# Two transformer layers on one core: the routing of the second mixture of experts moved into the second attention's loop

## Time and profile before

| what | value |
|---|---|
| median of 3 runs | 2520.67 us (2514.0 to 2524.66) |
| the profiled execution | 2512.72 us, its span 2511.0 us |
| layer0 | 0 to about 599 us |
| attention1 | about 600 to 1863 us, first scores at 619 us |
| route1 | about 1863 to 2126 us |
| experts1, combine1 | about 2127 to 2431 us, then to 2511 us |
| PE clock granted, mean | 0.92 of 2.4 GHz |

### The profile page before, as it was taken

How to read it: one execution, slowest core, us unless ns; L and a number is a source line. 1 busy time by engine, 2 the same in 40 slices (tenths; PEclk the granted TensorE clock), 3 DMA queues, 4 the chain that set the end, 5 groups by cost and what they waited for, 6 DMA issues and landing times. The chain is left out here.

```text
span 2511.0 us, 67688 instructions
## 1 busy us (share of the span) xinstructions
PE 2272.6 (91%) x16828; PEld 1709.2 (68%) x16829; DVE 1888.3 (75%) x6162; ACT 1605.6 (64%) x4162; POOL 1015.9 (40%) x1979
## 2 busy tenths in 40 slices
PE   5999999997999999999999999999989991999960
PEld 3777777774666666666666666666657771999960
DVE  6888888871888888888888888888864552666658
ACT  2555555553777777777777777777753331667664
POOL 5676676671222222222222222222213666555542
PEclk9999999997999999999999999999985555999985
DMA  1011001001000000000000000000021111222225
GB/s 33 28 31 33 30 29 33 27 26 47 1 0 0 0 0 0 0 0 0 0 0 0 0 0 0 0 0 0 0 70 61 58 62 52 57 60 60 61 69 168
DMA packets 77583, 68.83 MB, mean 27 GB/s; under 512 B 10573, under 2 KB 70490, under 8 KB 77036
## 3 DMA queue, kind: packets, MB, share of 16 engines
q1 hardware_dynamic: 68830, 50.88, 6.9%
q0 software_dynamic: 8704, 17.39, 2.1%
HBM read 33.55 MB, written 22.62 MB: 22 GB/s over the span
## 5 line engine op out<-in xcount | busy, mean ns | idle before, releaser
L1017 DVE SCALAR_TENSOR_TENSOR restT<-ps_t,leadT 128x512 f16<-128x512 f32 (+1 forms) x768 | 462.8, 603 | 147.3 <-ACT leadT L978 95.3
L892 PE MATMUL ps_s<-xT_all,qm 128*128 (+1 forms) x1024 | 492.8, 563 | 11.8 <-issue 10.9
L978 ACT ACTIVATE leadT<-ps_t 128x512 f16<-128x512 f32 (+1 forms) x768 | 400.4, 522 | 151.0 <-PE ps_t L908 151.0
L908 PEld LDWEIGHTS ps_t<-ident,p 128*128 128x128 f32 x2560 | 320.8, 141 | 216.4 <-issue 180.9
L908 PE MATMUL ps_t<-ident,p 128*128 128x128 f32 x2560 | 405.4, 273 | 1.2 <-DVE restT L1017 0.5
L846 POOL CAST v_parts<-v_all 128x36 bf16 (+1 forms) x256 | 56.3, 220 | 805.8 <-PE ps_o L921 805.8
L1008 DVE CUSTOM_DVE_ANT_0 ps_s<-ps_s,mask 128x512 f32<-128x512 f32 (+1 forms) x512 | 320.1, 625 | 46.7 <-PE ps_s L892 46.6
L970 ACT ACTIVATE p<-ps_s,neg_max 128x512 f32<-128x512 f32 (+1 forms) x512 | 323.5, 632 | 4.6 <-DVE neg_max L1008 4.1
L892 PEld LDWEIGHTS ps_low<-xT_all,qm 128*128 128x128 f32 x1024 | 195.1, 191 | 135.8 <-issue 122.5
L884 PE MATMUL ps_qm<-xT_all,m_head 128*128 (+1 forms) x512 | 275.2, 619 | 0.3 <-issue 0.3
L267 POOL TENSOR_TENSOR pv_prod<-probs,kv 128x2048 f32<-128x2048 f32 x64 | 259.6, 4080 | 0.1
(11 more groups left out here) (222 smaller groups left out, 4570.2 us busy)
## 6 DMA issues: line engine op xcount, KB each, us to landing
row_in<-rows_dram SPq DMA_DIRECT2D x136, 64.5 KB, 1.9
y<-results SPq DMA_DIRECT2D x32, 256.0 KB, 3.3
xT<-in_xT SPq DMA_DIRECT2D x32, 128.0 KB, 2.2
xres<-in_xT SPq DMA_DIRECT2D x32, 128.0 KB, 2.1
x_all<-x SPq DMA_DIRECT2D x32, 128.0 KB, 2.0
xT_all<-x2T SPq DMA_DIRECT2D x32, 128.0 KB, 2.0
x_all<-x SPq DMA_DIRECT2D x16, 256.0 KB, 2.3
out_x<-x SPq DMA_DIRECT2D x16, 256.0 KB, 2.2
```

The lines of the kernel that those rows point to most:

```text
L892: mm = pe.matmul(ps_s[n], qm[j][:, n * P:(n + 1) * P], xT_all[:, bass.ds(sequence(u) * S, (n + 1) * P)], start=True, stop=True)
L908: mm = pe.transpose(ps_t[g][:, at + n * P:at + (n + 1) * P], probs[i][:, n * P:(n + 1) * P], ident[:, :])
L978: act.activation(leadT[j][g][:, :], ps_t[g][:, 0:width[g]], ACT.Copy, scale=RAISE)\
L1017: dve.scalar_tensor_tensor(out=restT[j][g][:, :], in0=ps_t[g][:, 0:width[g]], scalar=RAISE, in1=leadT[j][g][:, :], op0=ALU.mult, op1=ALU.s ...
```

## The change

`route1` is gone as a stage. Its work is called from inside `attention1`'s loop, in one PSUM bank (`ps_r`) that the attention did not use, for the sequence before the one whose heads are being computed. Every engine, after its work for step (b, h) of the attention, runs `route(b - 1, h)`; which part runs at which h is written in each engine's `route`. The loop now runs over sequences, with all 16 heads of one in its body; the first two sequences and the last are written out, so head numbers, and offsets that depend on them alone, are constants. `sa_all` is gone: the attention of one sequence is held in `sa`, already in rows. `x_all` is written by the routing and not by `layer0` (L215's transfer and its waits go). The expert weights are loaded late over parts of `xT_all` and `v_all` that are done with.

The product with the reciprocal sums goes from DVE to POOL, between `load_head` and `split_values`.

The residual is a product with the identity: `x2T` (= xT_all of the group + bias, added on POOL) times `[I | 2(mean(c) - c)]`, and `saT` times `[Wp | Wp 2(mean(c) - c)]`, both accumulated into 136 columns: 128 of x2 + attention, and 8 that, scaled by the row's rstd, are the cross term of the distance. x3 itself is no longer turned. The sum of squares of a normalised row is taken as 128 var rstd^2, on POOL. Rows for the indirect transfers are made by ACT's normalisation directly (rank 0) and a copy on POOL (rank 1).

Part of the diff that the prediction speaks of (POOL, PE, DVE and ACT in the new `attention1`):

```diff
+                with eng.Fori(2, NG - 1) as b:
+                    for h in range(H):
+                        step(b, h, True, True, True, True)
+                        route(b - 1, h)
...
+                one(NG, 0)
+                one(NG, 1)
+                for h in range(2, H):
+                    route(NG - 1, h)
 # POOL
                 def step(b, h, nxt, last, this, older):
                     if nxt:
+                        load_head(*before(b, h, -1))
+                    if older:
+                        normalise(*before(b, h, 2))
+                    if nxt:
+                        split_values(*before(b, h, -1))
+
+                def route(g, h):
+                    if h == 2:
+                        bias_x2T(g)
+                    if h == 4:
+                        inverse(g, 0)
+                    if h == 7:
+                        inverse(g, 1)
+                    if h == 10:
+                        make_rows(g)
+                        keep_tops(g)
+                    if h == 13:
+                        scatter(g, range(0, 3))
+                    if h == 14:
+                        scatter(g, range(3, 6))
+                    if h == 15:
+                        scatter(g, range(6, 8))
...
+                def inverse(g, a):
+                    pool.wait_ge(moments, 2 * (n + 1))
+                    pool.tensor_tensor(var[a] <- moment[:, :, 1] + eps_pair)
+                    pool.tensor_scalar(negm[a] <- -moment[:, :, 0])
+                    pool.tensor_scalar(var_d[a] <- 128 * moment[:, :, 1])
+                    pool.tensor_tensor(rstd[a] <- var[a] ** minus_half)
+                    pool.tensor_tensor(shift[a] <- negm[a] * rstd[a])
+                    pool.tensor_tensor(rstd_sq[a] <- rstd[a] * rstd[a])
+                    pool.tensor_tensor(norm_sq[a] <- var_d[a] * rstd_sq[a])
+                    pool.tensor_tensor(added <- csq + norm_sq[a])
 # PE
+                    if this and h == 2 and not (isinstance(b, int) and b == 0):
+                        turn_sa(b - 1)
...
+                def project(g, a):
+                    pe.wait_ge(saT_sb, g + 1)
+                    pe.wait_ge(x2T_sb, g + 1)
+                    if a:
+                        pe.wait_ge(normed, B * g + 2)
+                    for i in range(2):
+                        pe.matmul(blk(ps_r, i, WD), blk(x2T, 2 * a + i), id_c[:, :], start=True, stop=False)
+                        mm = pe.matmul(blk(ps_r, i, WD), blk(saT, 2 * a + i), wp_c[:, :], start=False, stop=True)
...
+                def route(g, h):
+                    if h == 3:
+                        project(g, 0)
+                    if h == 6:
+                        project(g, 1)
+                    if h == 11:
+                        count(g)
 # ACT
+                def route(g, h):
+                    if h == 2:
+                        copy_saT(g)
+                    if h == 5:
+                        norm3(g, 0)
+                    if h == 8:
+                        norm3(g, 1)
 # DVE
+                def route(g, h):
+                    if h == 4:
+                        moments_of(g, 0)
+                    if h == 5:
+                        scale(g, 0)
+                    if h == 7:
+                        moments_of(g, 1)
+                    if h == 8:
+                        scale(g, 1)
+                    if h == 9:
+                        square_distances(g)
+                        find_tops(g)
+                    if h == 10:
+                        find_indices(g)
+                    if h == 11:
+                        pick(g)
+                    if h == 12:
+                        find_places(g)
```

More of the change, by code:

```diff
@@ L719, in layer0, with skewed, one, earlier @@
     nc.all_engine_barrier()
[L722 to L734, removed]
+def skewed(eng, n, begin, ahead, depth, stride, step):
+    def one(s):
+        step(s // stride, s % stride, lambda p: 0 <= s - p < n)
+    whole = (n - ahead - begin) // stride * stride
+    for s in range(begin):
+        one(s)
+    first, j0 = begin // stride, begin % stride
+    with eng.Fori(first, first + whole // stride) as u:
+        for j in range(j0, j0 + stride):
+            step(u + j // stride, j % stride, lambda p: True)
+    for s in range(begin + whole, n + depth):
+        one(s)
+def earlier(u, j, p, stride=2):
+    return u + (j - p) // stride, (j - p) % stride
+ROW = P + 1
+NOWHERE = 1 << 22
+def attention1(nc, sh, wqT, wkT, bq, wp, wpT, bp, bv1, cT, keep, routing, expert_loads):
+    xT_all, v_all, x_all, ident = keep
+    rows_dram, squares_all, tile_expert, tile_row = routing
+    S, B, NG = sh.seq, sh.blocks, sh.batches
+    NT, LIST, TILES = sh.tiles, sh.list_rows, sh.listed_tiles
+    NK = NG * H
+    WD = P + E
     PV = DH + 1
@@ L860, in _ @@
                 load_head(0, 0)
                 split_values(0, 0)
-                steps(step)(pool)
+                steps(step, route)(pool)
+                pool.wait_ge(pads_ready, 2)
+                for e in range(E):
+                    pool.indirect_dma_start(
+                        out=rows_dram[:, :], out_offset=bass.IndirectOffsetOnAxis(ap=pad_idx[:, e:e + 1], axis=0),
+                        in_=filler[:, :], in_offset=None).then_inc(pads_scattered, 16)
+                pool.wait_ge(scattered, 16 * 2 * B * NG)
@@ L864, in _ @@
+                pool.wait_ge(pads_scattered, 16 * E)
             @block.tensor
@@ L1060, in step @@
                     if this:
-                        mask_and_max(u, j, 2)
-                        mask_and_max(u, j, 1)
-                        mask_and_max(u, j, 0)
-                steps(step)(dve)
-def skewed(eng, n, begin, ahead, depth, stride, step):
-    def one(s):
-        step(s // stride, s % stride, lambda p: 0 <= s - p < n)
-    whole = (n - ahead - begin) // stride * stride
-    for s in range(begin):
-        one(s)
-    first, j0 = begin // stride, begin % stride
-    with eng.Fori(first, first + whole // stride) as u:
-        for j in range(j0, j0 + stride):
-            step(u + j // stride, j % stride, lambda p: True)
-    for s in range(begin + whole, n + depth):
-        one(s)
```

859 lines of the change are left out of this document (396 added, 463 removed).

## The result

The changed kernel takes 2629.97 us (median of 4 runs, 2623.95 to 2631.09), the kernel before 2517.93 us on the same chip: ratio 1.0437, 95% interval 1.0407 to 1.0467. It is 4.4% slower; 2640 us had been forecast.

What follows compares the result with a forecast made beforehand. PE bounds the attention, with POOL's chain to `queries` nearly as long; POOL's transfer issue bounds the routing. 2512.7 - 222 + 234 + 59 + 8 - 20 + 60 = 2631.7, with 8 for the median 2640 us; range 2500 to 2770.

Steps and rivals of the forecast that it cites:

- The centre: In the attention, PE waits for POOL's `m_head` at `queries` in seven heads of each sequence, some 15 us a sequence.
- The stage and the tail: Routing stage behind the attention: 259.8 us go, a tail of 38 us comes for the last sequence; net -222 us.
- POOL's routing: POOL's routing work between `split_values` and the next `load_head`, with 0.2 us of slack: 15.6 us a sequence, +234 us.
- PE's routing: Turning `sa`, `project` and `count` in the attention, PE having no idle time: 3.9 us a sequence, +59 us (50 to 75).
- DVE and ACT: Their routing work in the attention's heads: DVE 0.5 us a sequence, ACT's falls into idle time; +8 us (0 to 30).
- The loop: Attention loop with 16 constant heads a turn: up to 31 us go, against fetches of longer code; -20 us (-31 to +10).
- The clock: PE's clock falls after its idle times in heads with transfers and inverses: 4 us a sequence, +60 us.
- hidden: Rival: `m_head` has two buffers, so PE never waits at `queries` and POOL's work is hidden; 2346 us, chance 0.08.
- partial: Rival case: transfers in the attention at 0.96 us and no fall of the clock; 2526 down to some 2480 us, chance 0.09.
- the lower clock holds: Rival: PE's lower clock lasts through the routing heads, 12 or more us a sequence instead of 4; 2770 us, chance 0.17.
- DVE or code: Rival: DVE's added work or the long loop body's code in the attention; no separate size given, chance 0.06.

Runs made afterwards that it cites:

- the fastest kernel: Changed kernel with POOL's routing ahead of `split_values` and of the reciprocal product, transfers one a head, PE's `count` in head 12; 2363.73 us, 0.9308 to the kernel before.

## Why the prediction was right

The centre held: seven waits for `m_head` a sequence, longest in the heads with three transfers, 99.3 us a sequence (6.2 a head), plain heads at 4.69 to 4.80, 46 us from the last head to the first product of the experts (2240.65). By steps, a sequence meaning one of 15:

- *The stage and the tail*: 38 us forecast, 39.0 measured.
- *POOL's routing*: 15.6 a sequence forecast, 13.6 of waits measured (204.4 in all against 234). By head, in the sequence shown: `bias_x2T` 0.74 (0.9), `inverse` 1.81 and 1.79 (2.0), rows 0.69 (1.2), transfers 3.91, 3.30 and 0.99 (3.6, 3.6, 2.3); the second is between 3.10 and 3.91 from sequence to sequence. The last is short because DVE's idle time at the turn of the loop falls into the same head and holds PE up ahead of `queries`; 1.3 us of POOL's term are hidden under that of the loop.
- *PE's routing*: 3.9 forecast. From the intervals between `queries`, turning `sa` 0.44, the projections 1.03 and 0.93, the count with its wait of 1.1 for `pick` 1.73: 4.1, 62 us against 59.
- *DVE and ACT*: 8 us forecast; no row isolates them.
- *The loop*: -20 forecast; -4 by itself (0 to -8). This is the term that failed in kind. The forecast left 11 us for the long body against the 31 to be won, an allowance that no run shows; in its place 27 us were measured, 2.3 at each of 12 turns, with an idle time of DVE of 2.6 to 2.9 us that waits for nothing but its issue, and with three times the instruction packets. That the loop of before is not fetched again holds (no packet between 660 and 1830 us), but a loop of 4 heads can't show what a body of 16 does.
- *The clock*: 60 forecast, 4 a sequence. The mean granted clock in the loop was 0.96, so that at most 0.04 x 99.3 = 4.0 us a sequence went to it. The changed kernel's own sequences give 1.6 us for 3.4 us more at the lower clock; with 7.8 us of it in the mean sequence, that is 3.7. From another side: with the routing moved, a sequence (first to last turning of `sa`, over 15) takes (1989.4 - 716.0) / 15 = 84.9 us instead of (2195.6 - 706.3) / 15 = 99.3; 11.3 of these 14.4 are waits for `m_head`, and 3.1 are left for the clock and what comes with it. 45 to 60 us, then, in the size forecast.

So the sum met the time with two errors against each other: POOL's term 30 us too large, the loop's 16 too favourable. The mechanism was right; that the total came within 10 us is in part luck. Of the rivals, "hidden" fell by the waits themselves, "partial" by the clock, which did fall, and "the lower clock holds" by 0.96; of "DVE or code" the price of the long body did come, 27 us, and POOL's error hid it. But the hidden rival's figure was not absurd as a kernel: it is about what the same work costs where POOL is idle (2346 us forecast for it; 0.9308 x 2517.93 = 2344 in the fastest kernel; that the two are so near is chance). Its condition, that added work stays under the slack, was read for one place in POOL's order only; in the other the slack is 2.6 us a head.

## What to carry to other kernels

An engine that is busy a quarter of the time can still be on the critical path for most of its instructions: ask for each place in its order how long after it the next engine needs the result, and add work only where the engine itself is waiting for another. Before fusing a stage into a loop, write down that slack for every gap of a step, not for the step as a whole; the same instructions here cost 4.4% in one gap and brought 4.6% in the one beside it. And a wait's length isn't its price: moving products that waited 1.1 us gave 2.4 us a sequence by the runs, 3.1 in the two traces. Last, one sequence of a trace may not stand for all: here the clock fell once in some, twice or three times in others, and only all of them together gave its price.

## What the runs showed of the hardware that was not expected

- A loop body of 16 heads costs an idle time of DVE of 2.6 to 2.9 us at each turn and is fetched again, with five packets of 8 KB (148 and 143 instruction packets in all); one of 8 heads has no such idle time and moves no packet between 700 and 1815 us (58 in all); in the loops of 4 and 8 heads PE waits 0.2 us for its issue at a turn and loses 0.5 to 0.7 in all (mean intervals of 4.82 and 4.78 us against 4.70).
- In the loop an indirect transfer of 128 rows costs POOL mostly 0.4 to 0.6 us ahead of the first, 0.96 to 1.09 busy and 0.30 between two, the last two much as in the stage. With PE's `count` at the end of head 11 POOL waits 0.7 us or more between the last transfer and `split_values`, with `count` in head 12 not at all (0.9544 against 0.9402); why is open.
- In the changed kernel and in the one with the transfers one by one, the clock fell to its lower level behind every wait of PE of 3.48 to 4.07 us, behind those of 2.0 to 2.1 us in seven of 14 cases, and behind none of five of 3.10 to 3.30; it was back at full 3 to 7 us after the wait. In the changed kernel a sequence with 3.4 us more at the lower clock took 1.6 us longer.
